# A decoder layer on one core: order of the first tile's moves, queues of the late weights, and steps of the zeroing

## What is computed

```python
x = layernorm(x + attn(x))                 # 16 heads of 64, causal, proj_w, proj_b
x = layernorm(x + xattn(x, ctx, mask))     # 16 heads of 16 over 77 context tokens
x = layernorm(x + moe(x))                  # 8 experts, top 2, capacity 1280, fallback FFN

# attn: q, k, v = einsum('bxy,iyk->bxik', x, W).reshape(h, b, t, hs)
#       softmax(q k^T * hs**-0.5, causal) v, then .reshape(b, t, h*hs) @ proj_w.T + proj_b
# moe:  for each expert e: x_e = x[idx]; y_e = gelu(x_e @ W1[e] + b1[e]) @ W2[e] + b2[e]
#       y = y.at[idx].add(y_e * w); a token that overflows takes y_fb = ffn(x, fw1, fb1, fw2, fb2)
```

## Time and profile before

| | |
|---|---|
| median of 3 runs | 1508.05 us (1507.47 to 1509.12) |
| the profiled execution's own time | 1509.21 us |
| its span in the trace | 1507.5 us |
| mean granted clock of TensorE | 0.956 of full speed |
| PE busy | 1301.3 us (86%) |
| DVE busy | 1083.8 us (72%) |
| ACT busy | 924.1 us (61%) |
| POOL busy | 721.1 us (48%) |

### The profile page before, as it was taken

How to read it: one execution, slowest core, us unless ns; L and a number is a source line. 1 busy time by engine, 2 the same in 40 slices (tenths; PEclk the granted TensorE clock), 3 DMA queues, 4 the chain that set the end, 5 groups by cost and what they waited for, 6 DMA issues and landing times. The chain is left out here.

```text
span 1507.5 us, 47409 instructions
## 1 busy us (share of the span) xinstructions
PE 1301.3 (86%) x16821; PEld 1079.2 (72%) x16821; DVE 1083.8 (72%) x3112; ACT 924.1 (61%) x2287; POOL 721.1 (48%) x970
## 2 busy tenths in 40 slices
PE   3589999999999999999999999864899999999930
PEld 2478778778878877887887887632688888888820
DVE  4678888888888888888888888748455555555537
ACT  3566777778777777777877766514344444444426
POOL 3144564674565566566556644420243344343326
PEclk9899999999999999999999999995899999999975
DMA  9657767667657667676676664019333363333235
GB/s 222 145 138 161 171 169 160 137 145 175 142 140 184 132 140 190 130 150 155 154 154 142 153 105 90 24 61 421 125 75 76 75 163 93 80 75 77 70 139 206
DMA packets 293216, 208.95 MB, mean 139 GB/s; under 512 B 218782, under 2 KB 250654, under 8 KB 290560
## 3 DMA queue, kind: packets, MB, share of 16 engines
q1 hardware_dynamic: 281952, 184.01, 51.0%
q0 software_dynamic: 6816, 17.71, 4.1%
q10 hardware_dynamic: 4224, 4.19, 0.8%
HBM read 93.79 MB, written 65.93 MB: 106 GB/s over the span
## 5 line engine op out<-in xcount | busy, mean ns | idle before, releaser
L1729 PE MATMUL ps_e<-xt,wres 128*128 128x128 f16 x3408 | 343.5, 220 | 5.2 <-DMA xt<-xg 4.2
L1729 PEld LDWEIGHTS ps_e<-xt,wres 128*128 x3408 | 285.8, 99 | 77.1 <-issue 5.9
L1793 ACT ACTIVATE act_g<-ps_e,b 128x128 f32<-128x128 f32 x568 | 162.4, 369 | 208.1 <-PE ps_e L1729 206.3
L1736 PE MATMUL ps_e<-wres,g_hi 128*128 x568 | 214.5, 379 | 0.8 <-DVE g_lo L1816 0.8
L743 ACT ACTIVATE probs<-st_k,nmax 128x128 f32<-128x128 f32 (+1 forms) x512 | 199.9, 448 | 1.9 <-DVE nmax L964 1.6
L964 DVE CUSTOM_DVE_ANT_0 st_k<-ps,causal 128x128 f32<-128x128 f32 (+1 forms) x512 | 160.6, 351 | 38.0 <-PE ps L444 37.9
L1696 POOL DMA_INDIRECT z_scr<-e_y,dst_i x71 | 82.9, 1168 | 212.6 <-DVE e_y L1807 212.6
L750 ACT ACTIVATE pt_hi<-ps 128x384 f16<-128x384 f32 x256 | 125.2, 489 | 56.0 <-PE ps L452 27.7
L1738 PE MATMUL ps_e<-wres,g_lo 128*128 x568 | 154.8, 273 | 0.0
L452 PE MATMUL ps<-ident,probs 128*128 128x128 f32 x768 | 130.5, 279 | 24.4 <-ACT probs L743 19.3
L969 DVE TENSOR_TENSOR pt_lo<-ps,pt_hi 128x384 f16<-128x384 f32 x256 | 141.4, 552 | 6.0 <-ACT pt_hi L750 2.6
(11 more groups left out here) (281 smaller groups left out, 4044.9 us busy)
## 6 DMA issues: line engine op xcount, KB each, us to landing
k_pair<-k_pair SPq DMA_DIRECT2D x96, 256.0 KB, 6.6
st_p<-in_moe_w SPq DMA_DIRECT2D x24, 768.0 KB, 5.8
w_scr<-st_p SPq DMA_DIRECT2D x24, 768.0 KB, 4.1
wres<-w_scr SPq DMA_DIRECT2D x18, 1024.0 KB, 20.9
v_scr<-v_tok SPq DMA_DIRECT2D x32, 512.0 KB, 4.2
v_pos<-v_scr SPq DMA_DIRECT2D x64, 256.0 KB, 6.1
q_st<-st_q SPq DMA_DIRECT2D x64, 128.0 KB, 2.8
z_scr<-zero SPq DMA_DIRECT2D x32, 256.0 KB, 3.3
```

The source lines that it names most:

```text
L1729: last = mm(out, w(c * FF + f * P, b, P), xt[:, t % X_BUFS, a, c], start=(m == 0), stop=(m == 5))
L1736: mm(out[:, 0:2 * D], g_hi[:, t % G_BUFS, f], w(KC * FF + f * D, 0, 2 * D), start=(f == 0), stop=False, skip_group_check=True)
L1793: nc.scalar.activation(act_g[:, k % 2, f], ps[:, 3 + 2 * (k % 2) + f // 4, (f % 4) * P:(f % 4 + 1) * P], ACT.Gelu, bias=bias[:, f:f + 1], ...
```

## The change

Three things are changed, and no arithmetic. First, in step -1 SP issues the first tile's moves in another order: v_out, both key moves, query move, the first half of the low queries, the key double, the second half of the low queries, and `v_in` last. For later tiles the order is as before. Second, the weights that are split in step 0 are no longer loaded by SP: proj goes through ACT's queue, one half behind the split of v and one behind that of k; the four xw go through POOL's queue behind the constants. The causal mask's matmul and copies move from ahead of the first fill to the start of step -1. Third, `zeros` issues one of its 32 DMAs at the end of each of the 32 steps.

```diff
--- before.py
+++ after.py
@@ -56,7 +56,7 @@
 NF = len(FILLS)
 PAIRS = H // 2
 
-ZERO_STEPS = 4
+ZERO_STEPS = TILES
 V_LOADS = 2
 
 V_FILLS, K_FILLS = 3, 4
@@ -261,11 +261,7 @@
                 sp.dma_start(stage[n][:], io["w" + n].rearrange("(c p) n -> p c n", p=P)).then_inc(ld[n], 16)
             sp.dma_start(proj_b[:], io["proj_b"].rearrange("(a n) -> a n", a=1).partition_broadcast(P)[:, 0, :]).then_inc(s_small, 16)
 
-        def other_weights():
-            for half in range(2):
-                sp.dma_start(stage_p[half * HS:(half + 1) * HS], io["proj"].rearrange("(h d) n -> d h n", d=HS)).then_inc(ld["p"], 16)
-            for n in ("k", "v", "q", "o"):
-                sp.dma_start(stage_x[n][:], io["xw" + n].rearrange("(c p) n -> p c n", p=P)).then_inc(ld["x"], 16)
+        def small_weights():
             sp.dma_start(mask[:], io["mask"].rearrange("(c p) k -> p c k", p=P)).then_inc(s_small, 16)
             sp.dma_start(wr[:], io["wr"].rearrange("(c p) n -> p c n", p=P)).then_inc(s_small, 16)
 
@@ -314,10 +310,13 @@
             sp.wait_ge(s_fill_hi, NF * (t + 1))
             sp.dma_start(q_st[0:HS, p, :, 1], q_st[HS:P, p, :, 0]).then_inc(s_qmove, 16)
 
-        def query_low(t):
+        def query_low_first(t):
             p = t % 2
             sp.wait_ge(s_fill_lo, NF * (t + 1))
             sp.dma_start(q_st[HS:P, p, :, 1], q_low[HS:P]).then_inc(s_qlow, 16)
+
+        def query_low_second(t):
+            p = t % 2
             sp.wait_ge(s_qmove, 16 * (t + 1))
             sp.dma_start(q_st[HS:P, p, :, 0], q_low[0:HS]).then_inc(s_qlow, 16)
 
@@ -355,10 +354,18 @@
                 load_x(0)
                 load_x(1)
                 first_weights()
-                other_weights()
+                small_weights()
             if s >= 0 and has(s + 2):
                 load_x(s + 2)
-            if has(s + 1):
+            if s == -1:
+                v_out(0)
+                key_move(0)
+                query_move(0)
+                query_low_first(0)
+                key_double(0)
+                query_low_second(0)
+                v_in(0)
+            elif has(s + 1):
                 v_out(s + 1)
                 v_in(s + 1)
                 key_move(s + 1)
@@ -367,9 +374,10 @@
                 load_rows(s)
             if has(s) and even(s):
                 load_context(half(s))
-            if has(s + 1):
+            if has(s + 1) and s >= 0:
                 query_move(s + 1)
-                query_low(s + 1)
+                query_low_first(s + 1)
+                query_low_second(s + 1)
             if has(s - 2):
                 x2_out(s - 2)
                 pair_out(s - 2)
@@ -700,9 +708,11 @@
             if has(s + 2):
                 fill(s + 2, 3)
 
-        pe.wait_ge(s_const, N_CONST)
-        mm(c7[:, 0:P], ident_big, causal16, start=True, stop=True).then_inc(s_const, 1)
-        run(step)
+        def causal_mask():
+            pe.wait_ge(s_const, N_CONST)
+            mm(c7[:, 0:P], ident_big, causal16, start=True, stop=True).then_inc(s_const, 1)
+
+        run(step, {-1: causal_mask})
 
 
     @block.scalar
@@ -912,11 +922,20 @@
             if has(s + 1):
                 exps(s + 1, 1)
 
-        split_weights(0, FIRST)
-        act.wait_ge(s_const, N_CONST + 1)
-        for n in (0, 2):
-            nc.scalar.activation(causal[:, n], c7[:, 0:P], ACT.Copy).then_inc(s_const, 1)
-        run(step)
+        def causal_mask():
+            act.wait_ge(s_const, N_CONST + 1)
+            for n in (0, 2):
+                nc.scalar.activation(causal[:, n], c7[:, 0:P], ACT.Copy).then_inc(s_const, 1)
+
+        def projection_in(at):
+            act.dma_start(stage_p[at:at + HS], io["proj"].rearrange("(h d) n -> d h n", d=HS)).then_inc(ld["p"], 16)
+
+        split_weights(0, splits_until("v"))
+        projection_in(0)
+        split_weights(splits_until("v"), splits_until("k1"))
+        projection_in(HS)
+        split_weights(splits_until("k1"), FIRST)
+        run(step, {-1: causal_mask})
 
 
     @block.vector
@@ -1211,6 +1230,7 @@
                 nc.gpsimd.affine_select(out=head_rows[rows], in_=head_rows[rows], compare_op=ALU.is_ge, fill=0.0, base=DK - 1,
                                         pattern=[[DK, HB // 2], [0, CTX]], channel_multiplier=-1).then_inc(s_const, 1)
             pool.wait_ge(s_const, N_CONST)
+            late_weights()
 
         def value_constants():
 
@@ -1245,6 +1265,10 @@
                 pool.wait_ge(s_pv2, 2 * t)
             nc.gpsimd.tensor_tensor(v2_own[:, cc].rearrange("p s k d -> p s (k d)"), v2_rows[:, cc].rearrange("p s k d -> p s (k d)"),
                                     slot_heads[:].unsqueeze(2).to_broadcast([P, HEAD_SLOTS, 2 * (1 + DK)]), ALU.mult).then_inc(s_vown, 1)
+
+        def late_weights():
+            for n in ("k", "v", "q", "o"):
+                pool.dma_start(stage_x[n][:], io["xw" + n].rearrange("(c p) n -> p c n", p=P)).then_inc(ld["x"], 16)
 
         def split(pool, src, up, hi, lo, n, s_hi, s_lo):
```

## The result

| | before | after |
|---|---|---|
| median of the runs, us | 1508.05 (1507.47 to 1509.12) | 1498.97 (1497.96 to 1500.44) |
| profiled execution: own time / span, us | 1509.21 / 1507.5 | 1499.4 / 1497.7 |
| PE's idle ahead of the first scores, us | 16.4 | 8.1 |
| first scores on PE, us | 43.98 | 34.95 |
| SP issues `v_out` / the second key move, us | 21.73 / 30.92 | 20.59 / 23.02 |

The changed kernel is 9.1 us faster: ratio 0.994, 95% interval 0.9923 to 0.9957. The forecast was 1497.5 us in a range from 1493.5 to 1501.5 us; the measured median lies 1.5 us above it. The span fell by 9.8 us and the first scores came 9.0 us earlier.

What follows compares the result with a forecast made beforehand. In steady steps TensorE sets the time; at the start, from 23 us, only DMAs and their order hold PE. PE starts 10.5 us earlier, all else covered: 1508.05 - 10.5 = 1497.5 us, range 1493.5 to 1501.5 us.

Steps and rivals of the forecast that it cites:

- Keys ready, 22.97 + 1.1 us: DVE's low keys done at 22.97 us, plus delays: 0.6 us from proj beside q's load, 0.5 us from the mask.
- K, 27.9 to 31.7 us, taken 30: K is the time when both key moves of the first tile have landed; the middle, 30 us, was taken.
- the late end: Keys' 512 KB come on top of late weights and `v_out`, through at 28.75 us: both key moves landed at 31.7 us.
- the same engines: Rival: keys come through with the last late weights, PE starts 8.5 us earlier, 1499.5 us; chance 0.17.
- the early end: Second key move lands undisturbed, 3.1 us after its issue: both key moves landed at 27.9 us.
- K + 3.5 us to PE: PE's first scores follow the keys' landing by 0.1 + 0.6 (double's issue) + 2.8 us (last query move's landing).
- ACT stalls: Rival: ACT stalls issuing proj ahead of the q split, delaying all fills by 3.6 us: 1501.0 us; chance 0.08.
- Zeroing, 0: Steps 0 to 3 lose seven DMAs each, steps 4 to 31 gain one: gain 0, cost 0.
- The estimate of 4.9 us for a step: A later step must lose about 4.9 us on the chain of v, keys and queries before PE sees it.
- the sign of being wrong: The forecast is wrong if, among other signs, waits on query moves appear in steps 4 to 31; no size given.
- slower: Rival: spread zeroing delays v, keys, queries in steps 4 to 31, costing PE 0.5 us each: 1511.5 us; chance 0.03.
- the clock stays up: Rival: clock still up when PE resumes, up to 2.9 us more saved, 2.5 on the path: 1495.0 us; chance 0.25.

Runs made afterwards that it cites:

- experiment 1: The kernel before with only SP's new order of moves in step -1; late weights, mask and zeroing as before: 1501.22 us, ratio 0.9945.
- experiment 2: The kernel before with only the late weights moved to ACT's and POOL's queues; order, mask and zeroing as before: 1508.49 us, ratio 0.9995.
- experiment 3: The kernel before with only the zeroing spread over 32 steps: 1509.25 us, ratio 1.0.
- experiment 4: The changed kernel with the causal mask's matmul and copies back ahead of the first fill: 1498.67 us in a single execution.
- experiment 5: The changed kernel with proj's second half on SP behind `v_in(0)` and the four xw loads on POOL after the key moves landed: 1505.59 us, ratio 0.9981.
- experiment 8: The changed kernel with only the four xw loads held back until the last query move of tile 0 landed: 1499.09 us, ratio 0.9923.
- experiment 9: The changed kernel with xw held back as in experiment 8 and the mask ahead of the first fill as in experiment 4: 1496.55 us, ratio 0.9917.
- experiment 7: The changed kernel with three more 256 KB zeroing DMAs, into unread scratch, behind each of the 32: 1510.51 us, ratio 1.0017.
- Experiment 6: The changed kernel with 34 matmuls of 512 columns, results unread, ahead of PE's first scores: 1501.63 us, ratio 0.9944.

## Why the prediction was right, point by point

- **What bounds the start.** That the order of the moves on SP's queue is what counts held: experiment 1 gives 8.1 of the 9.1 us, experiments 2 and 3, the queues and the zeroing, nothing that can be told from zero. The mask's move was never run alone.
- **Keys ready, 22.97 + 1.1 us.** Too late by 1.8: DVE's low keys were done at 21.54 + 0.69 = 22.23 us. The delay of 1.1 us did not come as a whole. ACT's q split began 2.66 us behind its k split (2.50 before), so `proj` beside the `q` load cost 0.2 us and not up to 2.5. The mask did hold the last keys by 0.4 us (experiment 4), but this was outweighed: the first fill began 0.9 us earlier (11.74 against 12.60 us), and DVE was half a microsecond faster in its q split (last section), which the prediction had not counted.
- **K, 27.9 to 31.7 us, taken 30.** It was 30.9. This is the step that was mis-sized. The middle of the two ends had no ground of its own. From the moment that the keys were ready it allowed 30.0 - 24.1 = 5.9 us, and it took 30.9 - 22.2 = 8.7 us. That K is off by only 0.9 us is luck: the delay that didn't come hid most of the miss. Without it the ends would be 26.8 and 30.6 us, and the measured K stands at the late one. So the mechanism at work is that of the late end, the rival *the same engines*: first `v_out` and the last of the late weights land (29.3 and 29.0 us), then the keys. That rival had 17 in 100 and gave 1499.5 us, half a microsecond from the result. Experiments 5, 8 and 9, with loads held back, show what the early end is: 3.6 to 4.8 us in place of 7.9, not 3.1. Experiment 2, where the new queues alone gave nothing, says the same from the other side.
- **K + 3.5 us to PE.** 4.0 us: one issue as counted, and the last query move landed in 3.3 us, not 2.8. Sum of both terms: +0.9 and +0.5, the 1.45 us by which the scores came later than 33.5 us.
- **ACT's issues, 0.74 us each.** They took 0.72 and 0.61 us, beside ACT's own work; no stall as on SP. The rival *ACT stalls* falls. ACT's queue of the changed kernel, then POOL's:

```profile
7.78 0.72 ACTq L931 DMA_DIRECT2D st_p<-in_proj  x1
...
10.37 0.61 ACTq L931 DMA_DIRECT2D st_p<-in_proj  x1
```

```profile
13.11 0.97 POOL L1271 DMA_DIRECT2D st_xk<-in_xwk  x1 [0.32 <-POOL head_rows L1230]
```


- **POOL's four issues, 4 to 8 us, hidden.** 3.2 us (0.97 + 0.78 + 0.72 + 0.72), below the lower end; `split_x(1)` ran from 16.38 to 18.87 us, long before PE needed it.
- **`v_in` last, covered.** It left at 32.26 us; `pv` at 44.63 us waited for `pt_lo`. Held.
- **Zeroing, 0.** Held (experiment 3), and so did the slack in kind: experiment 7 finds its end. The estimate of 4.9 us for a step was too generous, though. In steps 6 to 31 the scores waited once, 0.2 us, before; in the changed kernel five times, 2.6 us in all and up to 1.0 us, in its repeat twice, 1.1 us in all. If these are waits for the moves (experiment 3), they are the sign of being wrong that the prediction named, in a size that the time doesn't show. The rival *slower* asked for 5.4 us on the chain for one DMA; four together cost PE 0.4 us.
- **The clock.** The case taken held: it had fallen when PE resumed. The rival *the clock stays up* counted 2.5 us for it on the path. Experiment 6 makes this case by force and gains nothing, so its price was wrong, beside its condition: what is won at the first scores is given back behind the next waits.
- **All behind step 0 shifts as a whole.** Nearly. From scores to scores steps 0 and 1 took 27.95 + 33.33 us against 27.54 + 33.06 before: 0.7 us given back. Behind step 1 the profiled execution gained 1.4 us more than that (span 9.8 us shorter, scores of step 2 8.35 us earlier), which lies within the scatter of its executions (1497.96 to 1500.44 us). The windows around the first `pv` and what follows it, of the kernel before and of the changed one (columns as above), show the clock down once more in the second, which goes with the 0.7 us; no run isolates it:

```profile
54.00:62.00 8.00, 5.49 (x84) 4.90 (x85) 7.45 (x26) 6.58 (x19) 0.00 (x0) 1.00 0.89 113
```

```profile
44.00:52.00 8.00, 6.88 (x83) 6.30 (x83) 6.03 (x20) 4.74 (x13) 0.00 (x0) 0.79 1.02 131
```


## What to carry to other kernels

When a small transfer on the critical path stands in a queue behind a wait for another transfer, move it ahead of that wait; this alone was nearly the whole gain. Moving bulk loads to other issuing engines didn't take them out of its way here: what it shares with them are the DMA engines, and to be quick there it needs the bulk loads issued later, behind the landing of the last small one, and only those that nobody needs soon. Before paying for a higher PE clock at one place, look at where PE idles next.

## What the runs showed of the hardware that was not expected

POOL's own tensor work slows DVE's; beside POOL's issuing of DMAs the same DVE instructions are faster. DVE's q split and what POOL did beside it, in the kernel of experiment 1 and in the changed kernel (start us, duration us):

```profile
14.54 3.16 DVE L943 SCALAR_TENSOR_TENSOR w_q<-st_q,w_q 128x512 f16<-128x512 f32 x4
```

```profile
12.78 1.16 POOL L1265 TENSOR_SCALAR x_up<-x_t 128x256 f32<-128x256 f32 x1
...
14.96 0.99 POOL L1269 TENSOR_TENSOR x_lo<-x_up,x_hi 128x256 f16<-128x256 f32 x1
```

```profile
14.46 2.48 DVE L950 SCALAR_TENSOR_TENSOR w_q<-st_q,w_q 128x512 f16<-128x512 f32 x4
```

```profile
14.85 0.72 POOL L1271 DMA_DIRECT2D st_xq<-in_xwq  x1
...
16.38 1.28 POOL L1277 TENSOR_SCALAR x_up<-x_t 128x256 f32<-128x256 f32 x1
```


The same four instructions take 3.16 us where POOL runs `split_x(1)` beside them, and 2.48 us where it issues loads until 16.3 us. In every kernel with the `xw` issues at that place it was 2.48 or 2.49 us (after and its repeat, 2, 4, 6, 7), in those without them 2.96 to 3.16 us (before, 1, 3, 5, 8, 9). It works the other way too: POOL's selects in the changed kernel took 0.49 us ahead of DVE's splits, 1.33 to 1.48 us beside those of v (128x1024) and 0.80 us beside those of k, whose instructions are half as long. The Trainium skill, "SBUF — State Buffer", section "SBUF: two separate sides", says that DVE and GpSimd share a pair of ports, that a DVE operation with two inputs in SBUF and a GpSimd operation that reads SBUF take it one after the other, each for its whole instruction, and that DMAs use other ports. These rows agree in direction; the price, 0.5 to 0.7 us of DVE for the four quarters of a split, is from here, and the prediction had left it out. With it `v_out` leaves at 20.59 us in place of 21.36 us in experiment 1. So what the queue move may be worth, and experiment 2 shows that alone it is too little to be measured, seems to lie in DVE's work and not in the transfers.
